# Graph-network layer on Trainium2: kept partial sums added to by adding transfers, eight rounds of unequal width, last round bank by bank

## The chip, the cores and the metric

One core of a Trainium2 chip runs the kernel. The metric is device time in microseconds (us) of the whole kernel, here of one launch on one core. The engines are PE (TensorE), DVE (VectorE), ACT (ScalarE), POOL (GpSimd) and SP (SyncE, which only issues transfers here). PEld is PE's weight load, which runs beside its products.

## The reference

12,500 nodes with 64 features, 400,000 edges (`src`, `dst`), three layers. Cut to what is computed:

```python
h = relu(layernorm(x))
for l in range(3):
    def mlp(z): return relu(z @ W1[l] + b1[l]) @ W2[l] + b2[l]
    msgs = mlp(h[dst])
    agg = segment_sum(msgs, src, num_segments=12500)
    h = mlp(h + agg)
out = x + h @ Wf + bf
```

A message depends only on the node it starts from, so each layer is a product of a matrix of edge counts (12,544 x 12,544 after padding) with the 12,544 messages, followed by the small MLP.

## The kernel before

**Counts.** The edge counts are small integers and are stored in device memory two to a byte (`counts_dram`). They are built once. The build has 49 columns of four groups, so 196 groups `k`. For each group DVE makes two one-hot tiles in `make_hots` (line 752: first the columns' tile, 128x832, here "cols", then the rows' tile, 128x4096, "rows"); POOL multiplies the first by the edges' weights (`weigh`, line 627); PE makes 32 small products (line 1307); ACT copies them out of PSUM (line 1132); DVE transposes the copy (line 760) two groups later; SP stores it. There are two slots for one-hots, so `make_hots(k)` waits until PE has used those of group k-2. Once every four groups, up to column 42, POOL also gathers edges for a later column (line 607).

**Layer 0.** The sums of layer 0 are made while the build runs. The result is split over seven stretches of 1792 nodes (a unit of work is one round for one stretch), each of four PSUM banks of 448 columns (one bank of one unit is called a job here). The build columns are taken in seven rounds of seven columns; round r needs the counts of its seven columns. A unit loads two chunks of counts from device memory (SP, line 450), DVE unpacks them into low and high halves (four instructions a unit, lines 791 and 799; 850 and 851 after the build), and PE multiplies: 14 products of 128x448 a job (line 1336). Between rounds the sum of each job is held in SBUF (`kept_sums`, in the tiles msg and arena): ACT copies it there (line 1141), and in the next round PE adds it back by a product with the identity in f32 (`add_kept`, line 1331) ahead of the job's own products. Unit u goes with build column u+8, one job a group, so that 41 of the 49 units run in the build; one more and the seven of the last round follow it. In these last ones the four banks run side by side over two chunks, and from the second stretch on PE also carries the MLP of the stretch before (`mlp_stage`, lines 1392, 1400, 1416) between them, ACT its activations (lines 1200, 1209, 1213), and DVE `read_sums` (lines 881 and 882, two instructions a bank) and `finish` (lines 894, 897).

**Layers 1 and 2** run from stored counts: seven stretches each, 5488 products in all on line 1438, with DVE unpacking (866, 867). The messages of each layer are scaled by their peak and split into two f16 parts (`upper_parts`, `lower_parts`); for layer 1 the peak goes through POOL (`share_peak`).

**Order.** All engines' programs are written out by hand in one order each; an engine runs its instructions in turn and waits on semaphores. SP's loads and stores share one queue.

The lines around which the change turns:

```python
if unit_of(j) >= 0:
    add_bank(unit_of(j), h)                    # PE, group k = 4j + h
t.matmul(ps[:, bank, 0:NB], ident[:], kept_sums(u % SB, b), start=True, stop=False)
```

## Time and profile before

| | us |
|---|---|
| Median of 3 runs (2256.7 to 2259.35) | 2258.89 |
| The profiled execution | 2256.61 |
| Its span | 2254.9 |
| up to the first rows' tile of the build | 64.1 |
| groups 0 to 31 of the build | 135.9 |
| groups 32 to 194, with layer 0 beside them | 742.9 |
| last group to the first product of the first whole unit after the build | 10.6 |
| two units without an MLP beside them | 28.7 |
| six stretches of the last round, with the MLP | 122.2 |
| layers 1 and 2 | 1150.5 |

A row of the timeline gives the start, the duration, the engine, the line of the kernel, the operation with what it writes and reads, and the idle time ahead of it with what ended that. Rows follow one another on an engine; a duration includes the fill and drain of the engine, so the pace of an engine is read from start to start.

### The profile page before, as it was taken

The page shows a single profiled execution, that of the slowest core. Times are in us where ns is not written, and L with a number is a line of the kernel's source. Part 1 is how long each engine was busy: PE and PEld are TensorE (multiplying, and loading weights), DVE is VectorE, ACT ScalarE, POOL GpSimd, SP SyncE. Part 2 cuts the span into 40 slices and gives each one's busy share as a digit, 9 for nine tenths or more (in the row PEclk, how much of TensorE's full clock was granted, in tenths as well). Part 3 has the DMA queues.
Part 4 walks back from the last instruction along what each step waited for, and adds up shares of the span by engine and source line. Part 5 has one row for each costly group of instructions (what it writes and reads, how often), then busy time and mean ns, then how long its engine had stood idle before and what let it go on. Part 6 is the DMA issues. An engine that isn't in the chain of part 4 may idle for free.

```text
span 2254.9 us, 39446 instructions
## 1 busy us (share of the span) xinstructions
PE 2096.7 (93%) x15866; PEld 1153.6 (51%) x15866; DVE 1512.7 (67%) x1683; ACT 663.7 (29%) x1632; POOL 643.7 (29%) x287
## 2 busy tenths in 40 slices
PE   3566779999999999999997999999999999999998
PEld 3444445555555555545553555555555555555554
DVE  7899999999999999846645434444463443444344
ACT  4885655555555555411200000000010000000000
POOL 3666667777767776500000000000000000000000
PEclk8796999999999999999998999999999999999999
DMA  7256666666666666642343435444444554555552
GB/s 194 71 139 180 178 181 189 182 188 196 190 188 193 185 187 176 186 125 72 122 127 110 146 111 160 151 128 145 143 132 134 157 165 126 169 159 159 145 157 68
DMA packets 332824, 344.46 MB, mean 153 GB/s; under 512 B 21562, under 2 KB 303992, under 8 KB 332184
## 3 DMA queue, kind: packets, MB, share of 16 engines
q1 hardware_dynamic: 327516, 335.59, 50.6%
q0 software_dynamic: 2352, 6.43, 1.1%
q8 instruction: 94, 1.54, 0.3%
q10 hardware_dynamic: 2816, 0.53, 0.2%
q14 instruction: 46, 0.38, 0.0%
HBM read 252.58 MB, written 89.89 MB: 152 GB/s over the span
## 4 chain that ended last, share of the span: by engine, by line
PE 80%; DVE 13%; issue 4%; DMA 2%; SPq 0%; ACT 0%; POOL 0%; DVEq 0%; POOLq 0%
PE ps L1438 46%; PE ps L1336 18%; DVE arena L752 6%; PE ps L1331 5%; PE ps L1307 5%; PE ps L1400 2%; DVE arena L760 2%; PE ps L1392 2%; PE ps L1416 1%; DMA arena<-counts_dram 1%; DVE arena L791 1%; DVE arena L799 1%; DVE arena L725 1%; SPq L439 0%; DVE msg L778 0%
## 5 line engine op out<-in xcount | busy, mean ns | idle before, releaser
L1438 PE MATMUL ps<-arena,parts 128*128 128x448 fp8e4 x5488 | 1054.0, 353 | 11.9 <-DVE arena L882 11.9
L1438 PEld LDWEIGHTS ps<-arena,parts 128*128 128x128 f16 x5488 | 535.1, 98 | 531.4 <-issue 44.7
L627 POOL TENSOR_TENSOR arena<-arena,weight_now 128x416 int32<-128x416 int32 x196 | 540.8, 2759 | 274.0 <-DVE arena L752 273.3
L866 DVE TENSOR_SCALAR arena<-arena 128x3136 uint16<-128x3136 uint16 x196 | 191.5, 977 | 624.5 <-PE ps L1438 617.9
L1336 PE MATMUL ps<-arena,parts 128*128 128x448 fp8e4 x2744 | 554.9, 353 | 1.5 <-DVE parts L832 1.5
L752 DVE TENSOR_TENSOR arena<-row_iota,key_now 128x4096 f16<-128x4096 f16 x196 | 446.3, 2277 | 0.0
L1336 PEld LDWEIGHTS ps<-arena,parts 128*128 128x128 f16 x2744 | 267.1, 98 | 296.9 <-issue 83.1
L1132 ACT ACTIVATE arena<-ps 128x800 uint16<-128x800 f32 x392 | 332.3, 874 | 73.2 <-PE ps L1307 64.1
L1200 ACT ACTIVATE arena<-ps,b1s 128x448 f32<-128x448 f32 x42 | 26.6, 634 | 943.5 <-PE ps L1392 943.5
L1307 PE MATMUL ps<-arena 128*128 128x53 fp8e4 x6272 | 204.3, 189 | 79.8 <-DVE arena L752 41.2
L1307 PEld LDWEIGHTS ps<-arena 128*128 128x128 f16 x6272 | 187.7, 98 | 151.4 <-DVE arena L752 95.5
L619 POOL COPY hT<-arena 128x896 f32 (+1 forms) x14 | 13.2, 945 | 699.5 <-ACT arena L1209 699.5
L760 DVE STREAM_TRANSPOSE arena<-arena 128x800 int32<-128x800 int32 x196 | 195.2, 996 | 3.7 <-DMA counts_dram<-arena 3.7
L867 DVE TENSOR_SCALAR arena<-arena 128x3136 uint16<-128x3136 uint16 x196 | 190.0, 969 | 0.0
L647 POOL PARTITION_ALL_REDUCE good<-good x1 | 0.4, 409 | 526.8 <-DVE good L1000 526.8
L752 DVE TENSOR_TENSOR arena<-word_iota,key_now 128x832 uint16<-128x832 f16 x196 | 113.5, 579 | 4.6 <-ACT weight_now L1111 4.6
L1141 ACT ACTIVATE msg<-ps 128x448 f32<-128x448 f32 x84 | 45.7, 544 | 163.7 <-PE ps L1336 163.7
L1331 PE MATMUL ps<-msg,ident 128*128 128x448 f32 x168 | 83.2, 577 | 3.0 <-DVE arena L851 3.0
L1331 PE MATMUL ps<-arena,ident 128*128 128x448 f32 x168 | 83.1, 576 | 0.0
L1141 ACT ACTIVATE arena<-ps 128x448 f32<-128x448 f32 x84 | 45.7, 544 | 118.9 <-PE ps L1336 118.9
L607 POOL DMA_INDIRECT arena<-edges_dram,start_i x49 | 76.5, 1562 | 8.0 <-issue 3.5
L791 DVE TENSOR_SCALAR arena<-arena 128x3136 uint16<-128x3136 uint16 x82 | 76.2, 930 | 3.1 <-DMA arena<-counts_dram 3.0
(127 smaller groups left out, 1146.9 us busy)
## 6 DMA issues: line engine op xcount, KB each, us to landing
arena<-counts_dram SPq DMA_DIRECT2D x294, 784.0 KB, 4.6
counts_dram<-arena SPq DMA_DIRECT2D x784, 100.0 KB, 2.2
h_dram<-parts SPq DMA_DIRECT2D x2, 1536.0 KB, 7.2
edges_dram<-arena SPq DMA_DIRECT2D x2, 1400.0 KB
arena<-in_x_dram SPq DMA_DIRECT2D x14, 192.0 KB
out_dram<-arena SPq DMA_DIRECT2D x14, 192.0 KB
arena<-in_dst_dram SPq DMA_DIRECT2D x1, 1400.0 KB
arena<-in_src_dram SPq DMA_DIRECT2D x1, 1400.0 KB
```

The costliest lines, as they stand in the source:

```text
L627: nc.gpsimd.tensor_tensor(pairs, pairs, weight_now[:, h * HW:(h + 1) * HW].unsqueeze(2).to_broadcast([P, HW, WORDS // 2]), ALU.mult).then_ ...
L752: return v.tensor_tensor(out, numbers.rearrange("p (m two) -> p m two", two=2).unsqueeze(1).to_broadcast(shape), key.unsqueeze(2).to_broad ...
L760: v.transpose(ctile[:, k % 2, :].bitcast(I32), stage[:, k % 2, :].bitcast(I32)).then_inc(s["counts_turned"], 1)
L791: v.tensor_scalar(spread[:, n % WIDE, 0, :].bitcast(U16), ring0[:, n % RING0, :].bitcast(U16), 0x0F0F, None, ALU.bitwise_and).then_inc(s[" ...
L866: v.tensor_scalar(spread[:, c % WIDE, 0, :].bitcast(U16), packed, 0x0F0F, None, ALU.bitwise_and)
L867: v.tensor_scalar(spread[:, c % WIDE, 1, :].bitcast(U16), packed, 4, 0x0F0F, ALU.logical_shift_right, ALU.bitwise_and).then_inc(s["counts_ ...
L1132: a.activation(to, product(q)[:, :, 0:2 * LP].rearrange("p c (m two) -> p c m two", two=2), ACT.Copy, scale=1.0 / WEIGHT_UNIT)
L1141: a.activation(kept_sums(u % SB, b), ps[:, bank, 0:NB], ACT.Copy).then_inc(s["sums_kept"], 1)
L1307: last = t.matmul(product(q)[:, c, 0:COLS], hot_r[:, slot, w, :], hot_c8[:, slot, w, 0:COLS], start=True, stop=True)
L1331: t.matmul(ps[:, bank, 0:NB], ident[:], kept_sums(u % SB, b), start=True, stop=False)
L1336: last = t.matmul(ps[:, bank, 0:NB], parts[:, (ROUND * (u // SB) + c) * CK + k, :], spread[:, c, b // 2, at:at + NB].bitcast(F8), start=u ...
L1438: last = t.matmul(ps[:, b, 0:NB], parts[:, c * CK + k, :], spread[:, c % WIDE, b // 2, at:at + NB].bitcast(F8), start=start, stop=stop)
```

## The change

Four things change in layer 0 and one at the start.

1. **Rounds.** There are eight rounds of 7, 7, 7, 7, 7, 6, 5 and 3 columns (`COLUMNS`), so 56 units and 224 jobs instead of 49 and 196. The number of products stays 2744. `spread_jobs` gives each of the first 196 jobs (`KEPT`) a build group: at most one seven-column job a group in round 0; then by a credit that gains 16 a group and pays twice the columns of a job. 179 jobs with 2406 products have a group of the build (before: 164 jobs with 2296), 17 of the seventh round follow it, then the 28 jobs of the last round. In rounds 1 to 4 every seventh or eighth group has two jobs (26 groups in all have two), and three or four groups at the start of rounds 2, 3 and 4 have none. DVE unpacks and SP loads by tables that follow from this (`unpack_group`, `load_group`): 180 unpacks in the build instead of 164; 26 groups have two.
2. **Kept sums.** PE no longer adds them. ACT copies a job's sum, scaled, into one of four stages (`sums_stage`), and POOL issues a transfer from that stage to the kept sum that adds (`add_sums`, `accum_op`). The 28 jobs of round 0 are copied to their kept place, and a transfer adds 64 rows of `hT` to each; 168 further transfers move 128 rows of 448 f32. A transfer of group k-1's job is issued behind `weigh(k)`, and ahead of the gather. `row_edges` becomes 8 bits wide, which makes room for the stages.
3. **Last round.** Its jobs are run bank after bank with six products each, with MLP stages between (`MLP_AT`). `read_sums` adds the kept sum in one instruction a bank, 28 instead of 56. Its first call waits for all adding transfers.
4. **Scale of layer 1.** The peak is turned and spread by two small products of PE rather than by POOL, after stretch 4's place in the order instead of after all.
5. **Start.** ACT keeps the first keys ahead of the square root and of `make_h0(0)`.

The diff, cut to its core:

```diff
+COLUMNS = (7, 7, 7, 7, 7, 6, 5, 3)
+ROUNDS = len(COLUMNS)
+FROM = [sum(COLUMNS[:r]) for r in range(ROUNDS + 1)]
 UNITS = ROUNDS * SB
-AHEAD = KG + 1
-FUSED = BUILD - AHEAD
+JOBS = UNITS * SBB
+KEPT = JOBS - SB * SBB
+CREDIT = 16
+STAGES = 4
...
+def spread_jobs():
+    groups, credit = [], 0
+    for k in range(BUILD * HG):
+        credit = 2 * KG if len(groups) < SB * SBB else min(credit, 2 * KG) + CREDIT
+        while len(groups) < KEPT:
+            r = len(groups) // (SB * SBB)
+            if k < HG * (FROM[r + 1] + 1) or credit < 2 * COLUMNS[r]:
+                break
+            credit -= 2 * COLUMNS[r]
+            groups.append(k)
+    return groups + [BUILD * HG] * (JOBS - len(groups))
+JOB_GROUP = spread_jobs()
+IN_LOOP = JOB_GROUP.index(BUILD * HG)
+def jobs_with(k):
+    return [n for n in range(IN_LOOP) if JOB_GROUP[n] == k]
+def unpack_group(n):
+    return max(JOB_GROUP[n - 1] if n else 0, JOB_GROUP[n] - 1)
+def load_group(n):
+    u, c = n // ROUND, n % ROUND
+    at = max(JOB_GROUP[u * SBB] - HG + c, HG * FROM[u // SB + 1])
+    if n >= RING0:
+        u, c = (n - RING0) // ROUND, (n - RING0) % ROUND
+        at = max(at, unpack_group(u * SBB + 2 + c) - 1)
+    return min(at, BUILD * HG)
...
-        row_edges = sb("row_edges", [P, BUILD * QN, QW], F16)
+        row_edges = sb("row_edges", [P, BUILD * QN, QW], U8)
+        sums_stage = sb("sums_stage", [P, STAGES, NB], F32)
...
+        def tiles_of(u, c):
+            n = COLUMNS[u // SB]
+            return 2 * FROM[u // SB] + c * n, n
...
+            for k in range(BUILD * HG):
+                if k in (3 * HG, 6 * HG):
+                    store_h0(k // (6 * HG))
+                while load_group(loaded) <= k:
+                    load_round(loaded)
+                    loaded += 1
+                store_counts(k)
+            for n in range(loaded, ROUND * UNITS):
...
+            def add_sums(n):
+                u, b = n // SBB, n % SBB
+                pool.wait_ge(s["sums_kept"], n + 1)
+                if u < SB:
+                    own = slice(b // 2 * D, b // 2 * D + D)
+                    pool.dma_start(kept_sums(u, b)[own], hT[own, u * SBH + b % 2 * NB:u * SBH + b % 2 * NB + NB],
+                                   accum_op=ALU.add).then_inc(s["rows_added"], 16)
+                else:
+                    if n == SB * SBB:
+                        pool.wait_ge(s["rows_added"], 16 * SB * SBB)
+                    pool.dma_start(kept_sums(u % SB, b), sums_stage[:, n % STAGES, :], accum_op=ALU.add).then_inc(
+                        sums_added[n % STAGES], 16)
...
+                for n in jobs_with(k - 1):
+                    add_sums(n)
...
+            def unpack_step(n):
+                u, c = n // SBB, n % ROUND
+                m = u * ROUND + c
+                size = tiles_of(u, c)[1] * SBH
+                packed = ring0[:, m % RING0, 0:size].bitcast(U16)
+                if n % SBB < 2:
+                    dve.wait_ge(round_loaded[m % RING0], 16 * (m // RING0 + 1))
+                    if u:
+                        dve.wait_ge(s["sums_done"], SBB * (u - 1) + 2)
+                    v.tensor_scalar(spread[:, c, 0, 0:size].bitcast(U16), packed, 0x0F0F, None, ALU.bitwise_and).then_inc(
+                        s["low_unpacked"], 1)
+                else:
+                    if u:
+                        dve.wait_ge(s["sums_done"], SBB * u)
+                    v.tensor_scalar(spread[:, c, 1, 0:size].bitcast(U16), packed, 4, 0x0F0F, ALU.logical_shift_right,
+                                    ALU.bitwise_and).then_inc(s["counts_unpacked"], 1)
...
+                    if l == 0:
+                        if i == 0 and b == 0:
+                            for added in sums_added:
+                                dve.wait_ge(added, 16 * (KEPT - SB * SBB) // STAGES)
+                        if i:
+                            dve.wait_ge(s["u_done"], 2 * (i - 1) + b % 2 + 1)
+                        v.scalar_tensor_tensor(zP[:, b * NB:(b + 1) * NB], ps[:, b, 0:NB], scal[:, 0, 6:7], kept_sums(i, b),
+                                               ALU.mult, ALU.add).then_inc(s["sums_read"], 1)
+                        continue
...
+            for n in range(unpacked, KEPT + SBB):
+                unpack_step(n)
+            for i in range(SB - 1):
+                n = KEPT + SBB * (i + 1)
+                read_sums(0, i, (0, 1))
                 if i >= 2:
                     finish(0, i - 2, 0)
+                unpack_step(n)
+                unpack_step(n + 1)
+                read_sums(0, i, (2, 3))
+                if i >= 2:
                     finish(0, i - 2, 1)
-                if i < SB - 1:
-                    unpack_tail(n + 2)
-            find_peak(1, BLOCKS + EARLY_PEAKS[1], EARLY_PEAKS[1])
+                    if 2 * (i - 1) == EARLY_PEAKS[1]:
+                        find_peak(1, BLOCKS + EARLY_PEAKS[1], EARLY_PEAKS[1])
+                unpack_step(n + 2)
+                unpack_step(n + 3)
+            reduce_peak(1)
+            make_scale(1)
+            finish(0, SB - 3, 0)
+            finish(0, SB - 3, 1)
+            lower_parts(1, 0)
             unpack(0, 1, 0, 0)
-            make_scale(1)
-            for n in range(4):
+            for n in range(1, 4):
...
+            act.wait_ge(s["variance_made"], 1)
+            a.activation(stat[:, 2, :], stat[:, 1, :], ACT.Sqrt).then_inc(s["root_made"], 1)
+            act.wait_ge(s["norm_made"], 1)
+            make_h0(0)
...
-            def keep_sums(u, b, bank):
-                act.wait_ge(s["sums_done"], SBB * u + b + 1)
-                if u < SB and b < 2:
-                    act.wait_ge(s["parts_made"], ROUND * (u + 1))
-                a.activation(kept_sums(u % SB, b), ps[:, bank, 0:NB], ACT.Copy).then_inc(s["sums_kept"], 1)
+            def keep_sums(n):
+                u, b = n // SBB, n % SBB
+                act.wait_ge(s["sums_done"], n + 1)
+                if u < SB:
+                    if b < 2:
+                        act.wait_ge(s["parts_made"], ROUND * (u + 1))
+                    to = kept_sums(u, b)
+                else:
+                    if n >= SB * SBB + STAGES:
+                        act.wait_ge(sums_added[n % STAGES], 16 * (n // STAGES - SB * SBB // STAGES))
+                    to = sums_stage[:, n % STAGES, :]
+                a.activation(to, ps[:, b % 2, 0:NB], ACT.Copy, scale=scal[:, 0, 6:7]).then_inc(s["sums_kept"], 1)
...
-            def add_kept(u, b, bank):
-                t.matmul(ps[:, bank, 0:NB], ident[:], kept_sums(u % SB, b), start=True, stop=False)
-            def multiply_chunk(u, c, b, bank, stop):
-                for k in range(CK):
-                    at = k * SBH + b % 2 * NB
-                    last = t.matmul(ps[:, bank, 0:NB], parts[:, (ROUND * (u // SB) + c) * CK + k, :],
-                                    spread[:, c, b // 2, at:at + NB].bitcast(F8), start=u < SB and c == 0 and k == 0,
-                                    stop=stop and k == CK - 1)
-                return last
-            def add_bank(u, b):
-                if b == 0:
-                    pe.wait_ge(s["parts_made"], ROUND * (u // SB + 1))
-                if SBB * u + b >= 2:
-                    pe.wait_ge(s["sums_kept"], SBB * u + b - 1)
+            def add_bank(n):
+                u, b = n // SBB, n % SBB
+                bank = b if n >= KEPT else b % 2
+                if n % (SB * SBB) == 0:
+                    pe.wait_ge(s["parts_made"], -(-2 * FROM[u // SB + 1] // CK))
+                if n < 2:
+                    pe.wait_ge(s["hidden0_kept"], BLOCKS)
+                elif n < KEPT:
+                    pe.wait_ge(s["sums_kept"], n - 1)
+                elif n < KEPT + 2:
+                    pe.wait_ge(s["sums_kept"], KEPT)
+                elif n == KEPT + 2:
+                    pe.wait_ge(s["scale_made"], 1)
+                elif n == KEPT + 3:
+                    pe.wait_ge(s["keys_kept"], 2 * BUILD)
                 else:
-                    pe.wait_ge(s["hidden0_kept"], BLOCKS)
-                if u >= SB:
-                    add_kept(u, b, b % 2)
+                    pe.wait_ge(s["sums_read"], n - KEPT - SBB + 1)
                 for c in range(ROUND):
+                    first, tiles = tiles_of(u, c)
                     pe.wait_ge(s["low_unpacked" if b < 2 else "counts_unpacked"], ROUND * u + c + 1)
-                    last = multiply_chunk(u, c, b, b % 2, c == ROUND - 1)
+                    for k in range(tiles):
+                        at = k * SBH + b % 2 * NB
+                        last = t.matmul(ps[:, bank, 0:NB], parts[:, first + k, :], spread[:, c, b // 2, at:at + NB].bitcast(F8),
+                                        start=c == 0 and k == 0, stop=c == ROUND - 1 and k == tiles - 1)
...
-            MLP_AT = {1: (0,), 2: (1,), 3: (2,), 5: (3,), 7: (4, 5)}
-            for u in range(FUSED, UNITS):
-                i = u - (UNITS - SB)
-                for c in range(ROUND):
-                    pe.wait_ge(s["counts_unpacked"], ROUND * u + c + 1)
-                    if c == 0 and u % SB == 0:
-                        pe.wait_ge(s["parts_made"], ROUND * (u // SB + 1))
-                    for b in range(SBB):
-                        if c == 0:
-                            if u == FUSED:
-                                pe.wait_ge(s["sums_kept"], SBB * FUSED if b < 2 else SBB * (FUSED - 1))
-                            elif i <= 0:
-                                pe.wait_ge(s["sums_kept"], SBB * FUSED + b + 1)
-                            else:
-                                pe.wait_ge(s["sums_read"], SBB * (i - 1) + b + 1)
-                            add_kept(u, b, b)
-                        last = multiply_chunk(u, c, b, b, c == ROUND - 1)
-                        if c == ROUND - 1:
-                            last.then_inc(s["sums_done"], 1)
-                        elif b == SBB - 1:
-                            last.then_inc(s["counts_used"], 1)
-                        if i >= 1:
-                            for n in MLP_AT.get(c * SBB + b + 1, ()):
-                                mlp_stage(0, i - 1, n)
+            MLP_AT = ((0, 1), (2,), (3,), (4, 5))
+            for n in range(IN_LOOP, JOBS):
+                add_bank(n)
+                i, b = n // SBB - (UNITS - SB), n % SBB
+                if i >= 1:
+                    for stage_n in MLP_AT[b]:
+                        mlp_stage(0, i - 1, stage_n)
+                if i == SB - 1 and b == 0:
+                    turn_peak(1)
+                if i == SB - 1 and b == 1:
+                    spread_peak(1)
```

POOL's queue in the build, at a place with one job a group and one with two. Before:

```order
L627 TENSOR_TENSOR arena<-arena,weight_now 128x32x13 [waits cols_made,keys_kept] x4
L607 DMA arena<-edges_dram,start_i 128x256 [waits keys_turned]
L627 TENSOR_TENSOR arena<-arena,weight_now 128x32x13 [waits cols_made,keys_kept] x4
L607 DMA arena<-edges_dram,start_i 128x256 [waits keys_turned]
L627 TENSOR_TENSOR arena<-arena,weight_now 128x32x13 [waits cols_made,keys_kept] x4
```

After:

```order
L671 TENSOR_TENSOR arena<-arena,weight_now 128x32x13 [waits cols_made,keys_kept]
L688 DMA msg<-sums_stage 128x448 [waits sums_kept]
L671 TENSOR_TENSOR arena<-arena,weight_now 128x32x13 [waits cols_made,keys_kept]
L688 DMA arena<-sums_stage 128x448 [waits sums_kept]
L651 DMA arena<-edges_dram,start_i 128x256 [waits keys_turned]
L671 TENSOR_TENSOR arena<-arena,weight_now 128x32x13 [waits cols_made,keys_kept]
L688 DMA arena<-sums_stage 128x448 [waits sums_kept]
L688 DMA msg<-sums_stage 128x448 [waits sums_kept]
L671 TENSOR_TENSOR arena<-arena,weight_now 128x32x13 [waits cols_made,keys_kept]
```

Behind each multiplication by the weights (line 671 now) stand one or two adding transfers that wait for ACT's copy, and the gather (line 651) stands behind them.

PE's queue in one stretch of the last round. Before:

```order
L1336 MATMUL ps<-arena,parts 128x448 x7
L1331 MATMUL ps<-msg,ident 128x448
L1336 MATMUL ps<-arena,parts 128x448 x7
L1392 MATMUL ps<-arena,W1s 64x448 x2
L1331 MATMUL ps<-msg,ident 128x448
L1336 MATMUL ps<-arena,parts 128x448 x7
L1392 MATMUL ps<-arena,W1s 64x448 x2
L1331 MATMUL ps<-arena,ident 128x448
L1336 MATMUL ps<-arena,parts 128x448 x7
L1400 MATMUL ps<-arena,W2b 128x448 x2
L1331 MATMUL ps<-arena,ident 128x448
L1336 MATMUL ps<-arena,parts 128x448 x14
```

After:

```order
L1419 MATMUL ps<-arena,parts 128x448 x6
L1465 MATMUL ps<-arena,W1s 64x448 x4
L1419 MATMUL ps<-arena,parts 128x448 x6
L1473 MATMUL ps<-arena,W2b 128x448 x2
L1419 MATMUL ps<-arena,parts 128x448 x6
L1473 MATMUL ps<-arena,W1b 128x448 x2
L1419 MATMUL ps<-arena,parts 128x448 x6
L1489 MATMUL ps<-W2b,arena 128x128 x7
```

The identity products (1331) are gone, and six products stand between two stages of the MLP.

ACT's queue at the start of the build. Before:

```order
L1087 ACT_TABLE_LOAD
L1087 ACTIVATE stat<-stat 128x98
L1092 ACTIVATE parts<-msg,stat 128x64 x8
L1100 COPY keys_row<-arena 128x256
L1101 ACTIVATE rk_now<-arena,row_base 128x128
L1109 COPY key_now<-ps 128x256
L1111 CAST weight_now<-ps 128x64
```

After:

```order
L1161 COPY keys_row<-arena 128x256
L1162 ACTIVATE rk_now<-arena,row_base 128x128
L1170 COPY key_now<-ps 128x256
L1172 CAST weight_now<-ps 128x64
L1170 COPY key_now<-ps 128x256
L1172 CAST weight_now<-ps 128x64
L1179 ACT_TABLE_LOAD
L1179 ACTIVATE stat<-stat 128x98
L1153 ACTIVATE parts<-msg,stat 128x64 x16
```

The keys (`keys_row`, `key_now`, `weight_now`), for which DVE's first one-hots wait, now come ahead of the normalisation (`stat`) and of h0 (`parts`).

## Rows read from the trace of the kernel before

**Rows 1.** Busy time by stage: stage, length, us (and instructions) of PE, PEld, DVE, ACT, POOL, clock, DMA share, GB/s.

```profile
199.93:942.86 742.93, 707.13 (x7880) 404.08 (x7878) 739.86 (x668) 434.95 (x1069) 513.40 (x198) 0.99 0.64 186
942.86:953.47 10.61, 7.62 (x64) 3.83 (x63) 6.89 (x8) 3.90 (x10) 2.83 (x1) 0.98 0.78 239
953.47:982.19 28.72, 28.72 (x129) 14.55 (x129) 10.37 (x13) 2.17 (x4) 0.00 (x0) 0.95 0.55 166
982.19:1104.39 122.20, 122.20 (x565) 62.17 (x565) 68.48 (x101) 27.49 (x45) 5.97 (x7) 1.00 0.29 88
```

**Rows 2.** Timeline, one group of the build, DVE and POOL.

```profile
604.13 0.58 DVE L752 TENSOR_TENSOR arena<-word_iota,key_now 128x832 uint16<-128x832 f16 x1
...
604.63 2.28 DVE L752 TENSOR_TENSOR arena<-row_iota,key_now 128x4096 f16<-128x4096 f16 x1
...
604.85 2.82 POOL L627 TENSOR_TENSOR arena<-arena,weight_now 128x416 int32<-128x416 int32 x1 [1.66 <-DVE arena L752]
...
606.83 1.00 DVE L760 STREAM_TRANSPOSE arena<-arena 128x800 int32<-128x800 int32 x1
...
607.76 0.93 DVE L791 TENSOR_SCALAR arena<-arena 128x3136 uint16<-128x3136 uint16 x1
...
608.61 0.58 DVE L752 TENSOR_TENSOR arena<-word_iota,key_now 128x832 uint16<-128x832 f16 x1
```

**Rows 3.** Chain that ended last, same group: start, us that it adds, what.

```profile
603.29 0.99 PE ps L1307 x32
604.29 0.84 PE ps L1331 x2
605.12 2.65 PE ps L1336 x14
```

**Rows 4.** Busy time by stage, early part of layer 0, no kept sums to add yet.

```profile
200.00:300.00 100.00, 75.79 (x940) 44.59 (x937) 99.19 (x94) 60.48 (x148) 67.67 (x26) 0.96 0.63 180
```

**Rows 5.** Timeline, PE and ACT in one stretch of the last round.

```profile
1043.29 0.92 PE L1331 MATMUL ps<-msg,ident 128*128 128x448 f32 x2
...
1044.04 1.49 PE L1336 MATMUL ps<-arena,parts 128*128 128x448 fp8e4 x7
...
1051.72 1.67 PE L1400 MATMUL ps<-arena,W2b 128*128 128x448 f32 x4
...
1052.67 1.39 ACT L1209 ACTIVATE arena<-ps,b2s 128x448 f32<-128x448 f32 x2 [2.38 <-PE ps L1400]
```

**Rows 6.** Timeline, POOL's gathers and DVE's instructions beside POOL, start of the run.

```profile
46.64 1.30 POOL L607 DMA_INDIRECT arena<-edges_dram,start_i  x1
...
47.06 0.17 DVE L714 TENSOR_SCALAR start_f<-start_f 128x7 f32<-128x7 f32 x1
...
47.53 0.38 DVE L714 TENSOR_SCALAR start_f<-start_f 128x7 f32<-128x7 f32 x1
...
49.50 0.95 POOL L607 DMA_INDIRECT arena<-edges_dram,start_i  x1 [0.30 <-issue]
...
66.28 1.29 DVE L752 TENSOR_TENSOR arena<-word_iota,key_now 128x832 uint16<-128x832 f16 x1
```

**Rows 7.** Timeline, a gather beside an unpack in the build.

```profile
616.73 0.93 DVE L799 TENSOR_SCALAR arena<-arena 128x3136 uint16<-128x3136 uint16 x1
...
616.80 1.70 POOL L607 DMA_INDIRECT arena<-edges_dram,start_i  x1 [0.16 <-issue]
```

**Rows 8.** Timeline, the first one-hot tile of the build.

```profile
63.57 0.59 DVE L752 TENSOR_TENSOR arena<-word_iota,key_now 128x832 uint16<-128x832 f16 x1 [4.64 <-ACT weight_now L1111]
```

**Rows 9.** DVE's waits, 190 to 945 us: us in total, times, longest.

```profile
DVE arena L791 <- DMA arena<-counts_dram: 3.0, 6, 0.8
```

**Rows 10.** The gathers' line: time from issue to landing.

```profile
DMA to landing us min/median/max: 2.5/4.7/6.6
```

**Rows 11.** Groups of instructions, 199.93 to 942.86 us: busy us, mean ns, idle before.

```profile
L1141 ACT ACTIVATE arena<-ps 128x448 f32<-128x448 f32 x80 | 43.5, 544 | 113.1 <-PE ps L1336 113.1
```

161 lines of the change are left out of this document (55 added, 106 removed).

## Prediction

> **What bounds the kernel now.** I read the busy times by stage first, to see which engine is never idle in each stage, then the timeline of one group and of one stretch, to see the pace from start to start, and then POOL's rows, since the change puts work on it.
>
> In the build with layer 0 beside it DVE is busy for 739.86 of 742.93 us [rows 1]. One group takes 4.48 us on DVE, start to start: 0.50 for the columns' tile, 2.20 for the rows' tile, 0.93 for the transpose, 0.85 for one unpack [rows 2]. PE needs as much: 0.99 for the counts' products, 0.84 for the kept sum, 2.65 for 14 products [rows 3]. The chain runs through PE there, but DVE has no gap either, so PE's relief alone cannot shorten a group. Behind the build PE is the bound: it is busy for all of 28.72 and 122.20 us, DVE for 68.48 of the last [rows 1]. There each us taken from PE counts until DVE, ACT or a wait comes up. POOL's multiplication lasts 2.82 us but mostly waits: it starts 0.22 us into the rows' tile and ends at 607.67, 0.76 after that tile's end at 606.91 [rows 2]. The work itself is some 0.76 us.
>
> **Start.** DVE waits 4.64 us for the first keys [rows 8]. They no longer stand behind ACT's eight h0 instructions, whose input DVE itself makes last. DVE can begin at once, but ACT is late next: it has 16 of these instructions in a row ahead of the first copies of counts. The bounds are 0 and -4.6; I take -3.5, near the wait shown, because ACT too begins earlier.
>
> **The build.** DVE's tiles and transposes stay. Unpacks: before 164 x 0.85 = 139.4 us. After: 140 of seven columns x 0.85 = 119.0, 28 of six and 12 of five. An unpack is 0.82 us for its bytes and 0.03 fixed by my split of 0.85 (estimate), so 0.735 and 0.62, which gives 20.6 and 7.4. In all 147.0, so **+7.6**. PE falls to 0.99 plus 8/7 x 2.65 = 4.0 us a group in rounds 1 to 4, against 3.63 + 8/7 x 0.85 = 4.60 on DVE: PE's 0.84 a group is hidden by DVE and worth nothing here. Two jobs in one group cost PE 0.99 + 5.30 = 6.3, once in seven or eight groups; two one-hot slots give it the slack of more than a group. PE's clock: with PE at 75.79% the granted share is still 0.96 [rows 4], at the upper level of 2.4 GHz nearly throughout, so only the three pauses of three or four groups without jobs can let it fall to 1.2 GHz, and PE's slack covers that.
>
> **POOL and its port.** POOL's queue becomes: multiply, one or two adding transfers, sometimes the gather. The next multiplication stands behind them. The trace has no adding transfer. A gather issues in 0.95 us alone [rows 6] and in 1.70 beside an unpack, ending at 618.50, 0.84 after the unpack's end at 617.66 [rows 7]. An adding transfer starts about 0.9 after the rows' tile ends, as this gather does, and ends 1.9 to 2.6 after it; two end by 3.6. POOL then waits for the next rows' tile anyway, which ends 4.6 later. So the issue itself is hidden; the cover is gone only above some 3.6 us of issue a group. What isn't hidden is what the port costs DVE, at two places.
>
> (a) In 26 groups DVE has two unpacks, in 23 of them with an adding transfer. If POOL gets its turn between them and holds on for all of its issue, the second unpack is 0.84 late: 23 x 0.84 = 19.3. If it holds on as in the row where a small DVE instruction took 0.38 beside a gather, against 0.17 for its like: 23 x 0.21 = 4.8 [rows 6].
>
> (b) In 32 groups the gather stands behind an adding transfer. If that ends later than the next columns' tile (2.27 after the rows' tile), the gather waits for the whole next rows' tile, and the multiplication behind it meets an unpack and then holds up the next columns' tile, which then takes 1.29 instead of 0.58 [rows 6, 2]: 32 x 0.71 = 22.7. By the ends above the gather comes at 2.05 to 2.8, so it is near either way; in the five groups with two transfers it surely is late: 5 x 0.71 = 3.6.
>
> Together the bounds are +8.4 and +42.0; nothing in it can give a gain. I take **+8.4**, since the only row of a DVE instruction beside a gather's issue shows a short hold.
>
> The Trainium skill speaks against the change here: "SBUF — State Buffer", section "Who interferes with whom", says that the pair of ports that DVE and GpSimd share is an exclusive lock held for the whole instruction, and the section on the two sides of SBUF that descriptors of GpSimd's transfers cannot be written while DVE runs in a two-port mode. The first agrees with the columns' tile of 1.29 us in the trace; for a transfer's issue it would make the term +42. It is the first rival below.
>
> **The transfers themselves.** 168 of 229 KB and 28 of half that in all, 164 whole ones' worth in the build. The DMA share is 0.64 at 186 GB/s there, so all 16 engines give some 291 GB/s and a whole one costs 0.79 us of them [rows 1]. That is 130 us on top of 475 in about 750: 0.81 busy. If reading the old sum too doubles the price, 0.98. DVE waits for loads for 3.0 us in six places now [rows 9]; I double that: **+3.0**. Loads are issued two groups ahead, 9 us.
>
> **Behind the build.** Now: 10.61 + 28.72 + 122.20 = 161.5 us from the last rows' tile to layer 1 [rows 1]. After:
> - the first stage as before, 10.6, since DVE's last transposes still wait for stores; one of the 17 late jobs falls in it
> - 16 jobs of ten products; 2.65 / 14 = 0.189 each [rows 3]: 30.2
> - 0.8 for ACT's last copy, 0.54 and the way there and back [rows 11]
> - the first stretch of the last round, 24 x 0.189: 4.5
> - the wait for the last adding transfer: copy 0.6, issue 0.95, landing 4.7 as a gather's median [rows 6, 10], and 0.5 for the read, less the 5.3 that lie beside it: 1.5
> - six stretches. One now takes 122.20 / 6 = 20.37 us [rows 1]; it loses 32 of 56 products (6.05) [rows 3] and four kept sums of 0.75, 1043.29 to 1044.04 (3.0) [rows 5]: 11.3 each, 67.9
> - DVE's queue ahead of layer 1 (scale, a finish, lower parts, an unpack, then the reads) is longer than the one stretch of PE beside it: 3.0, estimate
>
> That is 118.5, so **-43.0**. DVE is not the bound of a stretch: 68.48 / 6 = 11.4 now, less the eight read instructions that become four and four unpacks cut to 6/14. The scale by PE instead of POOL, and the 13 us in which DVE judges the counts after layer 1's first stretch, change nothing that PE waits for.
>
> **Sum.** 2256.6 - 3.5 + 7.6 + 8.4 + 3.0 - 43.0 = 2229.1 for an execution like the profiled one. That one lies 2.3 below the median of the runs, 2258.89, so 2231.
>
> **Rivals.**
> 1. *The port is held for all of each issue.* For it: the multiplication that waits for the rows' tile to the end, and the 1.29. Against: the 0.38. Both (a) and (b) at full price: 2231 + 33.6 = 2265, slower by 0.3%. It decides if the second unpack of a group is late by 0.84 rather than 0.2 and the gather falls behind the columns' tile.
> 2. *The adding transfers fill the DMA engines*, so that loads and stores land late and DVE waits in every group: slower. In the build (750 - 475) = 275 us of all engines are free for 164 transfers, 1.68 each, 2.1 times the plain price. At three times: 475 + 389 = 864, so 114 more: 2345. For it: a transfer that adds reads twice, and the share is 0.64 already. Against: the transfers lie within SBUF, in long rows of 1792 bytes.
> 3. *The stretches become a chain of hand-overs.* Between two stages of the MLP stood 7 to 14 products and a kept sum; now six products, 1.1 us. ACT finishes its pair 2.34 after the stage begins (1051.72 to 1054.06), PE's stage (1.67 with its drain) and six products take 2.6 to 2.8 [rows 5]. It is covered by 0.3 at least. If 0.8 shows at three hand-overs of six stretches, 14.4: 2246.
> 4. *PE's relief does shorten the build*, if DVE's start to start hides waits for PE: at most a few us, 2225. DVE's parts add up to the whole, so this has little for it.
>
> **How the numbers follow.** The forecast, 2231, 55%. Rival 1 14%, rival 2 11%, rival 3 13%, rival 4 and a cheaper start or tail 4%, other losses 3%. The range leaves out rival 2 and the far ends of the others: 2213 (start -4.6, no port or DMA cost, shorter waits in the tail) to 2267 (rival 1 with its spread). A measurement of this kernel tells 0.2%, 4.5 us, from no change. Faster by more: the forecast, rivals 3 and 4: 71%. Within: part of rivals 1 and 3: 8%. Slower: rival 2, the rest of rival 1 and other losses: 21%.
>
> **What would show it.** Groups of 3.63 + 0.85 per unpack on DVE in the build, unpacks of 0.93 with none near 1.8, and columns' tiles of 0.58 with few of 1.29; POOL idle ahead of most multiplications; last rows' tile near 955; stretches of 11 to 12 us with PE idle only ahead of the second; a DMA share in the build of 0.8 to 0.9. The prediction is wrong if columns' tiles or unpacks are stretched in most groups, if DVE waits for counts every group, or if PE is idle between the stages of the MLP.

## The result, and the profile after

Four runs of the changed kernel have a median of 2278.94 us (2276.58 to 2285.01), beside 2259.12 of the kernel before: a ratio of 1.0094, 95% interval 1.0073 to 1.0115. It is slower by 0.9%, where 2231 us and a gain of 1.2% were forecast; the time lies above the range. The profiled execution is the slowest of the four (2285.01, span 2283.2), 6.1 us above their median, and that of the kernel before lies 2.5 below its own; so 8.5 us of the difference between the two traces, 28.3, belong to these two executions.

Busy time by stage of the changed kernel, columns as in [rows 1]: up to group 32 of the build, the build from there with layer 0 beside it, the last transposes, the 16 late jobs, the first stretch of the last round, the rest up to layer 1, layers 1 and 2.

```profile
0.00:197.47 197.47, 103.82 (x1328) 88.24 (x1328) 176.96 (x285) 135.72 (x411) 113.11 (x71) 0.81 0.55 144
197.47:997.10 799.63, 639.93 (x7725) 381.51 (x7722) 766.84 (x682) 455.58 (x1085) 609.15 (x374) 0.94 0.89 222
997.10:1010.30 13.20, 7.38 (x67) 3.91 (x66) 6.64 (x8) 4.54 (x10) 6.32 (x5) 0.95 1.07 272
1010.30:1044.36 34.06, 33.29 (x160) 16.22 (x161) 11.19 (x17) 10.14 (x16) 13.52 (x15) 0.92 0.97 223
1044.36:1053.26 8.90, 4.70 (x25) 2.28 (x25) 2.94 (x7) 0.00 (x0) 0.98 (x1) 1.00 0.84 191
1053.26:1127.33 74.07, 68.68 (x329) 36.46 (x330) 44.73 (x80) 28.42 (x46) 5.59 (x6) 0.98 0.29 90
1127.33:2283.20 1155.87, 1131.62 (x5910) 584.68 (x5910) 508.19 (x611) 58.72 (x94) 8.33 (x10) 0.99 0.46 139
```

The build takes 799.63 us where it took 742.93 [rows 1]. Two columns say why. DVE is busy 27.0 us longer, 766.84 for 739.86. And it is now idle for 32.8 us, where it was for 3.1. The DMA share has gone from 0.64 to 0.89. Behind the build the four rows add up to 130.2 us, from 161.5.

The last row is 5.4 us longer than before, and 3.0 of these lie at the very end. There POOL goes through a closing drain, an instruction of its sequencer, and the kernel ends 0.24 us after it. First of the changed kernel, then of the kernel before (the number is its duration in ns):

```profile
L159 POOLq DRAIN  x1: 7073/7073/7073, 2275.9 to 2275.9; - x1
...
L113 POOLq DRAIN  x1: 4074/4074/4074, 2250.6 to 2250.6; - x1
```

DVE's groups of instructions in the build, shapes apart, and its wait for loads (us in total, times, longest):

```profile
L856 DVE TENSOR_SCALAR arena<-arena 128x3136 uint16<-128x3136 uint16 x69 | 73.5, 1071 | 28.2 <-DMA arena<-counts_dram 27.9
L861 DVE TENSOR_SCALAR arena<-arena 128x3136 uint16<-128x3136 uint16 x70 | 70.0, 1000 | 0.0
...
DVE arena L856 <- DMA arena<-counts_dram: 32.2, 27, 3.9
```

The seven-column unpack averages 1.07 and 1.00 us, not 0.93; and the six waits of 3.0 us of before [rows 9] have become 27 of 32.2. The timeline of DVE shows such a wait:

```profile
519.24 1.00 DVE L821 STREAM_TRANSPOSE arena<-arena 128x800 int32<-128x800 int32 x1
524.18 0.98 DVE L856 TENSOR_SCALAR arena<-arena 128x3136 uint16<-128x3136 uint16 x1 [3.93 <-DMA arena<-counts_dram]
```

The DMA queues in the build, first of the changed kernel, then of the kernel before: q0 carries what POOL issues (packets, MB, share of 16 engines); then issues, KB each, median us to landing.

```profile
q0 software_dynamic: 25038, 41.46, 30.6%
...
counts_dram<-arena SPq DMA_DIRECT2D x652, 100.0 KB, 3.6
arena<-counts_dram SPq DMA_DIRECT2D x68, 784.0 KB, 7.3
msg<-sums_stage POOLq DMA_DIRECT2D x74, 224.0 KB, 6.0
```

```profile
q0 software_dynamic: 1680, 4.59, 2.3%
...
counts_dram<-arena SPq DMA_DIRECT2D x652, 100.0 KB, 2.2
arena<-counts_dram SPq DMA_DIRECT2D x81, 784.0 KB, 5.2
```

Queue q0 holds 30.6% of 799.6 us, or 244.7 us of all 16 engines; the gathers held 2.3% of 742.9, or 17.1. The build has 148 whole adding transfers and 28 half ones, so 162 whole ones: (244.7 - 17.1) / 162 = 1.40 us each, where the prediction had 0.79. A load takes 7.3 us to land, from 5.2; a store 3.6, from 2.2. Their packets themselves are no slower: the loads' packets of 896 bytes take 0.048 us on average in both kernels, the stores' of 3200 bytes 0.176 before and 0.171 now. So the loads and stores are late because they queue. ACT, which must wait for a free stage, does so only twice, 3.3 us in all.

Why some unpacks are long is in the timelines of POOL (first four rows) and DVE in one group:

```profile
212.37 0.83 POOL L683 DMA_DIRECT2D msg<-hT  x1 [1.47 <-ACT msg L1211]
213.50 2.67 POOL L651 DMA_INDIRECT arena<-edges_dram,start_i  x1 [0.30 <-issue]
216.17 0.93 POOL L671 TENSOR_TENSOR arena<-arena,weight_now 128x416 int32<-128x416 int32 x1
217.00 1.05 POOL L683 DMA_DIRECT2D arena<-hT  x1
...
212.93 2.29 DVE L813 TENSOR_TENSOR arena<-row_iota,key_now 128x4096 f16<-128x4096 f16 x1
215.13 1.01 DVE L821 STREAM_TRANSPOSE arena<-arena 128x800 int32<-128x800 int32 x1
216.06 1.88 DVE L856 TENSOR_SCALAR arena<-arena 128x3136 uint16<-128x3136 uint16 x1
```

The adding transfer's issue puts the gather behind the next columns' tile. The gather starts inside the rows' tile, so it stands until the tile has ended (215.22) and ends 0.95 later, at 216.17. The multiplication behind it starts just when DVE starts its unpack, which takes 1.88 us, 0.95 too long: the multiplication's own 0.93. In the build 17 of DVE's instructions (15 unpacks, two columns' tiles) are stretched by over 0.3 us, 15.5 us in all. Beside each of them runs a multiplication; in 14 cases it stands directly behind a gather, and 12 of these gathers had waited for a rows' tile as this one did. Gathers that start just ahead of a rows' tile, by 0.03 us say, take 1.07 us and wait for nothing.

The issue of an adding transfer by itself hardly stretches anything of DVE's. Here one lies inside a rows' tile, POOL's row and DVE's:

```profile
482.17 0.91 POOL L688 DMA_DIRECT2D msg<-sums_stage  x1 [1.48 <-ACT sums_stage L1211]
...
482.12 2.29 DVE L813 TENSOR_TENSOR arena<-row_iota,key_now 128x4096 f16<-128x4096 f16 x1
```

Neither is longer than alone. Of the 139 seven-column unpacks, 93 have an issue and nothing else of POOL's beside them: they take 0.945 us on average (1.10 at most), and 0.952 the 29 with nothing beside them. But an unpack holds up the issue. Here the issue starts 0.14 us ahead of the unpack, POOL's row and DVE's:

```profile
236.02 1.18 POOL L683 DMA_DIRECT2D arena<-hT  x1
...
236.16 0.93 DVE L856 TENSOR_SCALAR arena<-arena 128x3136 uint16<-128x3136 uint16 x1
```

In 42 such cases (the issue up to 0.2 us ahead) every issue ends 0.10 to 0.13 us after the unpack. Issues with no unpack beside them take 0.87 us on average; the 79 that end in this way 1.07.

Behind the build, PE's timeline: the 16 late jobs, the first two stretches, and two later ones, which start 11.55 us apart; last DVE's first read of kept sums.

```profile
1010.30 33.29 PE L1419 MATMUL ps<-arena,parts 128*128 128x448 fp8e4 x160 [5.27 <-DVE arena L856]
1044.36 4.70 PE L1419 MATMUL ps<-arena,parts 128*128 128x448 fp8e4 x24 [0.77 <-ACT sums_stage L1211]
1053.26 2.25 PE L1419 MATMUL ps<-arena,parts 128*128 128x448 fp8e4 x6 [4.20 <-DVE arena L856]
...
1077.31 1.30 PE L1419 MATMUL ps<-arena,parts 128*128 128x448 fp8e4 x6
...
1088.86 1.30 PE L1419 MATMUL ps<-arena,parts 128*128 128x448 fp8e4 x6
...
1051.42 1.28 DVE L936 SCALAR_TENSOR_TENSOR arena<-ps,scal,msg 128x448 f32<-128x448 f32 x2 [5.97 <-DMA arena<-sums_stage]
```

### The profile page after: what moved, and what is told of

The parts are those of the page before. It is cut to its first block, busy times and chain, and to the rows that moved or that the text cites. A ratio compares the mean times of both kernels' runs of the same rounds, so it can differ in the third digit from the quotient of the medians.

```text
span 2283.2 us, 39388 instructions
## 1 busy us (share of the span) xinstructions
PE 1989.4 (87%) x15534; PEld 1113.3 (49%) x15534; DVE 1517.5 (66%) x1684; ACT 693.1 (30%) x1660; POOL 757.0 (33%) x482
## 4 chain that ended last, share of the span: by engine, by line
PE 57%; DVE 22%; DMA 9%; issue 7%; SPq 3%; POOL 1%; ACT 1%; DVEq 0%; POOLq 0%; ACTq 0%
PE ps L1511 45%; DVE arena L813 11%; DMA arena<-counts_dram 8%; DVE arena L821 4%; PE ps L1419 4%; SPq L489 2%; PE ps L1473 2%; DVE arena L861 2%; DVE arena L856 2%; PE ps L1465 2%; DMA counts_dram<-arena 1%; PE ps L1489 1%; PE ps L1374 1%; POOL arena L671 1%; DVE arena L786 1%
## 5 line engine op out<-in xcount | busy, mean ns | idle before, releaser
L1511 PE MATMUL ps<-arena,parts 128*128 128x448 fp8e4 x5488 | 1056.0, 354 | 15.5 <-DVE arena L946 11.9
L921 DVE TENSOR_SCALAR arena<-arena 128x3136 uint16<-128x3136 uint16 x196 | 191.5, 977 | 622.6 <-PE ps L1511 622.2
L1419 PE MATMUL ps<-arena,parts 128*128 128x448 fp8e4 x2744 | 569.0, 361 | 12.6 <-DVE arena L856 10.9
L671 POOL TENSOR_TENSOR arena<-arena,weight_now 128x416 int32<-128x416 int32 x196 | 481.1, 2455 | 149.5 <-DVE arena L813 145.7
L1374 PE MATMUL ps<-arena 128*128 128x53 fp8e4 x6272 | 212.9, 192 | 212.9 <-DVE arena L813 90.0
L1374 PEld LDWEIGHTS ps<-arena 128*128 128x128 f16 x6272 | 198.4, 100 | 277.1 <-DVE arena L813 221.0
L922 DVE TENSOR_SCALAR arena<-arena 128x3136 uint16<-128x3136 uint16 x196 | 190.2, 970 | 0.0
L1211 ACT ACTIVATE sums_stage<-ps,scal 128x448 f32<-128x448 f32 x168 | 106.7, 635 | 197.1 <-PE ps L1419 193.6
L856 DVE TENSOR_SCALAR arena<-arena 128x3136 uint16<-128x3136 uint16 (+3 forms) x112 | 107.0, 965 | 51.5 <-DMA arena<-counts_dram 41.3
L861 DVE TENSOR_SCALAR arena<-arena 128x3136 uint16<-128x3136 uint16 (+3 forms) x112 | 97.8, 887 | 3.9 <-PE ps L1419 3.9
L688 POOL DMA_DIRECT2D arena<-sums_stage x84 | 85.2, 1014 | 41.1 <-ACT sums_stage L1211 36.9
L688 POOL DMA_DIRECT2D msg<-sums_stage x84 | 80.0, 952 | 52.1 <-ACT sums_stage L1211 47.3
L1197 ACT ACTIVATE row_edges<-ps 128x16 uint8<-128x16 f32 x392 | 74.5, 190 | 0.0
```

The source lines that it names most:

```text
L671: nc.gpsimd.tensor_tensor(pairs, pairs, weight_now[:, h * HW:(h + 1) * HW].unsqueeze(2).to_broadcast([P, HW, WORDS // 2]), ALU.mult).then_ ...
L688: pool.dma_start(kept_sums(u % SB, b), sums_stage[:, n % STAGES, :], accum_op=ALU.add).then_inc(sums_added[n % STAGES], 16)
L856: v.tensor_scalar(spread[:, c, 0, 0:size].bitcast(U16), packed, 0x0F0F, None, ALU.bitwise_and).then_inc(s["low_unpacked"], 1)
L861: v.tensor_scalar(spread[:, c, 1, 0:size].bitcast(U16), packed, 4, 0x0F0F, ALU.logical_shift_right, ALU.bitwise_and).then_inc(s["counts_un ...
L921: v.tensor_scalar(spread[:, c % WIDE, 0, :].bitcast(U16), packed, 0x0F0F, None, ALU.bitwise_and)
L922: v.tensor_scalar(spread[:, c % WIDE, 1, :].bitcast(U16), packed, 4, 0x0F0F, ALU.logical_shift_right, ALU.bitwise_and).then_inc(s["counts_ ...
```

## The experiments

Line numbers of the experiments' rows are those of their own kernels. Medians are of four to ten runs; the kernel before, on the same chips, has 2258.0 to 2259.5.

**Theories.** 1: the adding transfers fill the DMA engines, and DVE waits for loads. 2: POOL's new work holds the port that it shares with DVE; either each issue does so (2a), or only the gather that is now late does, with the multiplication behind it (2b). 3: the schedule of eight rounds itself costs the time.

### No adding transfers

```diff
 def add_sums(n):
-    u, b = n // SBB, n % SBB
-    pool.wait_ge(s["sums_kept"], n + 1)
...
+    pass
```

> The changed kernel with all 196 adding transfers left out, and the waits for them (the sums kept between rounds and the own rows' hT are not added, so part of the computation is missing); everything else, the schedule of eight rounds, the unpacks and the last round bank by bank, stays. Theory 1 (the adding transfers fill the 16 DMA engines, so that loads land late and DVE waits for them, and part of the stretched instructions is contention): the build falls from 799.6 us to about 750, DVE's waits for loads from some 30 us to 3, and the whole to about 2225. Theory 2 (POOL's issue holds the port that it shares with DVE): the same total, about 2230, since the issues are gone too; this run alone doesn't tell 1 from 2. Theory 3 (the schedule itself, its bursts of jobs and pauses of PE, costs the time): the build stays near 790 and the whole near 2275.

2223.43 us, ratio 0.9839 (0.9822 to 0.9855). The build and the stages up to layer 1:

```profile
197.77:952.12 754.35, 625.41 (x7723) 375.44 (x7721) 747.11 (x683) 455.14 (x1085) 511.44 (x198) 0.96 0.66 187
...
952.12:1069.56 117.44, 109.79 (x581) 58.11 (x580) 65.57 (x109) 43.52 (x72) 8.43 (x7) 1.00 0.40 121
```

Theory 3 falls. Without the transfers the change is worth 1.6%, the tail is 117.4 us and DVE's busy time 747.1. The transfers as a whole cost 55 us. Between the two traces the difference is 61.5, of which 19.7 us are DVE's busy time and 25.6 its idle time in the build, 12.8 lie behind the build, and 3.0 in POOL's drain at the end, which takes 4.07 us here as in the kernel before. What is left of theory 3 is 4 us: DVE waits 7.2 us for loads here, 3.0 before. It does so in five places, four of them 122 to 128 us apart (337, 459, 586 and 714 us), as the rounds are.

### Few bytes, or a copy in place of an addition

```diff
-pool.dma_start(kept_sums(u % SB, b), sums_stage[:, n % STAGES, :], accum_op=ALU.add).then_inc(
+pool.dma_start(kept_sums(u % SB, b)[:, 0:32], sums_stage[:, n % STAGES, 0:32], accum_op=ALU.add).then_inc(
```

(and the same for hT)

> The changed kernel, but each adding transfer moves only the first 32 of 448 columns of its rows (the other columns are not added, so part of the computation is missing). The number of transfers, their issues on POOL, their waits and the number of descriptors stay; the bytes fall to 1/14. Theory 1 (bytes on the DMA engines): DVE's waits for loads fall from some 30 us to below 8, the DMA share of the build from 0.89 to about 0.70, the unpack of seven columns keeps its 1.07 us; the build is some 25 to 30 us shorter than 799.6, the whole about 2250. Theory 2 (the port is held during POOL's issue): the stretched unpacks and the rest of DVE's extra 19 us of busy time stay, whatever becomes of the waits. If instead the unpacks fall to 0.93 as well, they are stretched by the transfers' traffic and not by their issue, and the whole comes near 2230. If reading and writing cost by descriptor and not by byte, the DMA share stays above 0.8 and nothing much is gained.

```diff
-pool.dma_start(kept_sums(u % SB, b), sums_stage[:, n % STAGES, :], accum_op=ALU.add).then_inc(
+pool.dma_start(kept_sums(u % SB, b), sums_stage[:, n % STAGES, :]).then_inc(
```

> The changed kernel, but the 168 transfers of kept sums copy where they added (the old sum is overwritten and lost, so part of the computation is missing); the 28 of hT still add. Bytes moved, issues and waits stay. Theory 1 in the form of its price (an adding transfer takes the DMA engines 1.39 us where a copy of the same bytes takes 0.79, because the old sum is read too): the queue of these transfers falls from 30.7% of the build to about 18%, the DMA share from 0.89 to about 0.77, DVE's waits for loads from some 30 us to below 10, the whole to about 2255. If the transfers cost the same without adding, it is the bytes and descriptors from SBUF to SBUF that cost, and the whole stays at 2279. Theory 2 (the issue holds the port): no difference, 2279, in either case.

Few bytes: 2251.34 us (ratio 0.9945 to 0.9973). Copies: 2254.53 (0.9962 to 0.9989). The build of each, and q0 in the build with copies:

```profile
195.94:975.21 779.27, 633.66 (x7718) 378.10 (x7719) 771.73 (x683) 453.87 (x1085) 605.35 (x374) 0.95 0.69 185
```

```profile
196.25:974.55 778.30, 630.39 (x7720) 377.03 (x7718) 766.25 (x683) 455.10 (x1085) 592.01 (x374) 0.96 0.77 229
...
q0 software_dynamic: 13328, 41.53, 17.2%
```

With few bytes the waits are gone (779.27 - 771.73 = 7.5 us, with no transfer at all 7.2), but DVE's busy time is even 5 us longer: 25 stretched instructions, some 24 us. The copies leave waits of 11.9 us, somewhat more than the 10 expected. So the bytes make the waits, and something that remains makes the stretching. Theories 1 and 2 both hold, each for about half of the build's loss.

The copies give the price. By the queue's account they move the same bytes, at 17.2% of the build for 30.6%: (0.172 x 778.3 - 17.1 - 14 x 1.40) / 148 = 0.66 us for a copy, 1.40 for an addition. The Trainium skill, "Collectives: The Full Stack", section "The bandwidth ceiling: the fold count and why AG ≠ RS ≠ AR", says of collectives that an adding transfer is slow because it has two sources to read, with two read descriptors per chunk on one ring, and gives a ratio of 1.93. The ratio of prices here, 2.1, agrees.

The number of packets, 25,038 for 13,328, shows something else. An adding transfer has one packet for each of its rows, 1792 bytes and 0.176 us on average; a copy has packets of two or three rows, 3584 bytes in 0.162 us and 5376 in 0.232. Smaller packets alone don't explain the price: the loads' packets of 896 bytes take 0.048 us, so two of them would move a row in 0.10 (an estimate, since they come from device memory). Most of the difference therefore goes with the adding. That its reason is the reading of the old sum is not shown by itself, since the profile counts the same bytes for both.

### The start alone

```diff
-            act.wait_ge(s["norm_made"], 1)
-            make_h0(0)
...
             keep_keys(0, 1)
...
+            act.wait_ge(s["norm_made"], 1)
+            make_h0(0)
```

> The kernel before with one part of the change alone: ACT's order at the start, the square root and h0 behind the first keys. Nothing is left out. If the gain at the start is kept (the first rows' tile ends 5.6 us earlier in the changed kernel, but at group 32 only 2.5 us of it are left), 2256.6, that is 2.5 us below the kernel before; by the prediction's term 3.5 below, 2255.6. If the seven rounds of before take it back fully, 2259.

2254.58 us, ratio 0.9985 (0.9976 to 0.9995): 3.6 below the kernel before, with an interval of 1.1 to 5.4. The prediction's -3.5 lies well inside. In the trace much of the gain is lost on the way: the first rows' tile starts 5.9 us earlier than before, that of group 32 4.6, the last one 2.3, and the span is 2.5 shorter.

### The gather ahead of the adding transfers

```diff
 weigh(k)
-for n in jobs_with(k - 1):
-    add_sums(n)
 if k % HG == 2 and k // HG + WR < WT:
     gather(k // HG + WR)
+for n in jobs_with(k - 1):
+    add_sums(n)
```

> The changed kernel with one pair of steps exchanged in POOL's queue: in every fourth group the gather of the next window stands ahead of the adding transfers of that group, not behind them. Nothing is left out. Background: in the changed kernel 13 gathers of the build start late, wait through a whole rows' tile of DVE, and the multiplication behind each falls beside an unpack, which then takes 1.87 us where 0.94 is its own (14 to 15 us in all; 23 us with short transfers). Theory 2b (the late gather and the multiplication behind it hold DVE up, and the issue of an adding transfer by itself holds nothing): the stretched unpacks go, DVE's busy time in the build falls from 766.8 to about 750, the build by 12 to 16 us, the whole to about 2265. Theory 2a (any issue of POOL's beside an unpack stretches it): the stretching only moves to the adding transfers behind the gather, 2279. The waits for loads (some 30 us) stay or grow by some us under both, since the DMA engines have the same work in less time.

> The gather ahead of the adding transfers, and these move only the first 32 of 448 columns (the other columns are not added, so part of the computation is missing). It answers to the run with short rows alone, 2251.3 us, and to the run without any transfer, 2223.4. Theory 2b (late gathers hold DVE up, issues don't): nearly all that was left goes, DVE's busy time in the build falls from 771.7 to about 749, the whole to about 2228. Theory 2a (any issue beside an unpack stretches it): it stays near 2250. What lies between 2223.4 and this run is then the price of 196 issues, waits and descriptors with hardly any bytes in them.

> The changed kernel with the gather ahead of the adding transfers of its group, and the 168 transfers of sums copy where they added (the old sum is lost, so part of the computation is missing); bytes written, issues and waits stay. It completes the square: with the gather late, adding 2278.9, copying 2254.5, hardly any bytes 2251.3; with the gather first, adding 2276.5, hardly any bytes 2230.2. If the DMA engines are full only when the old sum is read too, so that the late gathers' cost was hidden behind them, this run gains the whole price of the late gathers: 2234 to 2238. If a copy's bytes alone fill them already, the waits for loads come up as they did with the gather first and adding, and it stays at 2248 to 2254.

With whole additions 2276.53 us, with few bytes 2230.16, with copies 2241.91. The builds, in this order:

```profile
195.06:987.67 792.61, 640.39 (x7721) 380.28 (x7722) 753.95 (x682) 456.42 (x1086) 619.00 (x374) 0.95 0.89 224
```

```profile
194.93:953.61 758.68, 628.04 (x7724) 375.37 (x7721) 750.98 (x682) 456.21 (x1085) 612.75 (x374) 0.96 0.71 190
```

```profile
196.33:960.10 763.77, 628.45 (x7723) 376.89 (x7721) 750.70 (x682) 455.06 (x1085) 603.39 (x374) 0.96 0.78 233
```

Theory 2b holds for the stretching, and 2a falls. The exchange of two steps takes 12.9 us from DVE's busy time with whole additions, 15.6 with copies and 20.8 with few bytes, though the same number of issues stays. With whole additions 4 stretched instructions are left of 17. One gather of the build, with DVE's unpack a little later, shows the cure:

```profile
209.78 1.61 POOL L651 DMA_INDIRECT arena<-edges_dram,start_i  x1 [0.17 <-issue]
211.39 0.93 POOL L683 DMA_DIRECT2D msg<-hT  x1
...
214.60 0.93 DVE L856 TENSOR_SCALAR arena<-arena 128x3136 uint16<-128x3136 uint16 x1
```

But the time of the first run missed its forecast of 2265: the gain is 2.4 us, inside the intervals. In the two traces the build is 7.0 us shorter, not 12.9. DVE's waits for loads rose from 32.2 us to

```profile
DVE arena L856 <- DMA arena<-counts_dram: 38.0, 30, 2.7
```

and the share stayed at 0.89. The copies came to 2241.9, between the two values on record for them (2234 to 2238 and 2248 to 2254). The six runs in one table, medians in us:

| | whole additions | copies | few bytes |
|---|---|---|---|
| gather behind the adding transfer | 2278.9 | 2254.5 | 2251.3 |
| gather ahead of it | 2276.5 | 2241.9 | 2230.2 |
| gain | 2.4 | 12.6 | 21.1 |

The fuller the DMA engines (0.89, 0.77, 0.69), the less a faster DVE gains: 2.4 of 12.9 us, 12.6 of 15.6, and all of 20.8. With whole additions it asks for its loads sooner, and waits 5.8 us more in the trace; the other 4.6 us between 7.0 and 2.4 are no more than the spread of the runs. With both causes away only 6.7 us are left against the kernel without transfers, and 2.9 of them are POOL's drain (6.95 us for 4.07). So neither loss can be read off by undoing the other.

### PE adds part of the sums

The gather first; PE adds the kept sum in jobs that stand alone in their group, 83 of 151 in one kernel and 99 in the other. `uS` holds a scaled identity here.

```diff
+if n in BY_PE:
+    t.matmul(ps[:, bank, 0:NB], uS[:, 0:P], kept_sums(u % SB, b), start=True, stop=False)
```

> The changed kernel with the gather first, and with PE adding the kept sum back (a product with a scaled identity, as the kernel before does it) in 83 of the 151 jobs of the build that add; ACT then copies the result straight to its place. 85 adding transfers of sums stay, in the groups with two jobs and behind the build, and the 28 of hT. Nothing is left out. Theory 1 and 2b together (each adding transfer costs the DMA engines 1.39 us, and PE has some 0.6 us a group to spare): the DMA share of the build falls from 0.89 to about 0.79, DVE's waits for loads from some 30 us to 10 or less, the build from 799.6 to about 760 us; the whole to about 2240, below the kernel before. Theory 3 (PE is the next bound: 0.84 us for each kept sum in a group, on top of bursts of two jobs): DVE waits for sums in its unpacks, the build stays above 780 and the whole near 2260.

> The same with PE adding in all 99 jobs that stand alone in their group; 69 adding transfers of sums stay. Nothing is left out. From the sums of PE (0.99 + 2.65 + 0.84 = 4.48 us for a group with one job, as much as DVE, and 6.3 for one with two) PE falls up to 9 us behind DVE's tiles before each pause, where it is up to 7 in the kernel with 83. If the DMA engines are what counts, this gains 2 to 4 us more than that kernel, about 2237. If PE is the bound, its time behind DVE shows as DVE's waits for sums in the unpacks, and it is slower than that kernel, 2245 to 2260.

Both 2253.4 us (ratios 0.9981, interval 0.9970 to 0.9992, and 0.9980, 0.9969 to 0.9990): better than both kernels, but not the 2240 and 2237 that were expected. The build and the tail of the first, whose profiled execution is the slowest of its ten (2260.7):

```profile
195.07:973.17 778.10, 691.33 (x7891) 410.11 (x7889) 754.10 (x682) 452.48 (x1086) 557.57 (x292) 0.96 0.78 205
...
973.17:1102.28 129.11, 114.36 (x579) 58.96 (x578) 65.41 (x109) 42.80 (x70) 25.28 (x26) 0.96 0.57 147
```

The share falls to 0.78 as forecast. The waits for loads fall to 19.4 us, not to 10, 4 us of waits for PE come up, and the tail keeps its 129 us, since its jobs still use transfers. In the second kernel the share is 0.75, the waits for loads are 15.9 us and those for PE 4.4, and the time is the same: the 16 transfers less bring nothing that shows. At the same share of 0.78 the copies with the gather first waited 13.0 us, this kernel 19.4, in 18 places all over the build. Why so much waiting is left with half of the transfers is not shown; of the adding transfers that stay in the build, most (52 in both kernels) belong to the groups with two jobs, where they stand close together.

### A version that beats both

The kernel before with the new start. ACT scales the sixth round's sums as it copies them, 28 half-size adding transfers add hT late in the build, and in the last round DVE adds the kept sum as it reads.

```diff
-                            add_kept(u, b, b)
+                            if i < 0:
+                                add_kept(u, b, b)
...
+                    if l == 0:
+                        v.scalar_tensor_tensor(zP[:, cols], ps[:, b, 0:NB], scal[:, 0, 6:7], kept_sums(i, b),
+                                               ALU.mult, ALU.add).then_inc(s["sums_read"], 1)
```

> A version built on the kernel before: its seven rounds and PE's adding back of the kept sums in rounds one to five, with the changed start order, and of the rest of the change only what takes work from PE behind the build. ACT scales the sums of the sixth round as it copies them; 28 adding transfers of half size put the own rows' hT to them, late in the build; in the last round PE no longer adds the kept sum, DVE adds it as it reads (four instructions a stretch where there were eight). Nothing is left out. What is saved: seven stretches lose four kept sums of 0.75 us each, 21 us, and the start gives 3.6 (the run of it alone). What it costs by the finding that an adding transfer's bytes on the DMA engines matter: 14 whole ones' worth of 1.39 us in a build with a DMA share of 0.64, hardly a wait. So about 2234, faster than the kernel before by 1.1%, and than the changed kernel by 2.0%. If the adding transfers as such (their issue, their waits) are what makes the changed kernel slow, it comes to 2245 or more; if PE is not the bound behind the build, to 2254.

2237.99 us, ratio 0.9908 (0.9892 to 0.9925): faster than the kernel before by 0.9%, than the changed one by 1.8%. The build and the stages up to layer 1, and PE at two points one stretch apart:

```profile
195.73:940.50 744.77, 707.67 (x7880) 404.34 (x7878) 740.12 (x668) 436.50 (x1069) 537.62 (x219) 0.99 0.66 188
940.50:1082.31 141.81, 137.31 (x700) 70.40 (x699) 69.45 (x96) 34.14 (x59) 15.23 (x15) 0.98 0.46 134
```

```profile
1032.19 0.97 PE L1415 MATMUL ps<-arena,W1s 128*64 128x448 f32 x4
...
1049.37 0.97 PE L1415 MATMUL ps<-arena,W1s 128*64 128x448 f32 x4
```

A stretch takes 17.18 us where it took 20.37, and the tail 141.8 for 161.5. The build is 1.8 us longer than before: 28 small transfers at a share of 0.66 cost little there (4.6 us of waits for loads, from 3.0). They cost 2.3 us in POOL's drain at the end, 6.36 for 4.07.

## Why the prediction was wrong

The step that failed is the price of the adding transfers: on the DMA engines (+3.0, which came to +29.2) and, by what an issue pushes behind it in POOL's queue, on DVE (+8.4, which came to +19.7). The tail added a smaller miss. In the order of the prediction's steps, with what each measured:

- **What bounds the kernel.** Right: DVE in the build, PE behind it. What the sum lacked is a third bound, the DMA engines, which it saw (share 0.64) and priced too low.
- **Start, -3.5.** Right, as far as it can be told: -3.6 by the run of it alone, 1.1 to 5.4.
- **Unpacks, +7.6.** Right: the kernel without transfers has 747.11 us of DVE's busy time for 739.86, +7.3.
- **Port, +8.4 taken of +8.4 to +42.** The term came to +19.7. The failing step is the choice between the ends. Part (a), the issue between two unpacks, did not happen: an issue holds nothing of DVE's and is itself held by the unpack, so 0.38 against 0.17 [rows 6], which lay beside a gather, was the wrong likeness. Part (b), the gather behind the adding transfer, happened as described and at more than its price: the multiplication mostly met the unpack itself, 0.95 us, and only twice a columns' tile. The text had called it near either way and counted 5 of 32; 12 came, and two more multiplications behind gathers that had not waited. These 14 and three others make 15.5 us; the other 4 are small amounts that no single row explains. Rival 1 expected both parts at full price; (b) came, (a) did not. The page that it cites (the Trainium skill, "SBUF — State Buffer", section "Who interferes with whom") tells of a lock held for the whole instruction. The trace agrees for the multiplication, whose whole 0.93 us are in the unpack's 1.88, but not for an issue: where it starts first, it does not hold the unpack. The prediction's other sentence from that page, that descriptors of POOL's transfers can't be written while DVE runs in a two-port mode, agrees with the 42 issues that end 0.10 to 0.13 us after the unpack.
- **DMA lateness, +3.0.** The largest miss in the build: +29.2 (waits 32.2 for 3.0), of which 25 go with the bytes and 4 with the schedule, where they stand without any transfer. The term rested on 0.79 us for a transfer, from a mean rate. It is 1.40, where a copy is 0.66. The text allowed for that ("0.98 if doubled"), yet let the waits only double. Rival 2 set its deciding point at 2.1 times 0.79 us, where the mean share reaches one. But waits grow long before that. In the kernel before they are 3.0 us at a share of 0.64. With the new schedule they are 7.2 at 0.66, 7.5 at 0.69, 7.7 at 0.71, 11.9 at 0.77, 13.0 and 19.4 at 0.78 (the copies with the gather first, and PE adding in 83 jobs), 32 to 38 at 0.89. That it is the bursts of jobs, loads and stores that make it so is argued, not shown.
- **Tail, -43.0.** -31.3; without transfers -44.1, so the terms for PE's work were right (stretches of 11.55 for 11.3). Missed: 2.6 in the first stage, where the DMA share is shown as 1.07 and DVE waits 3.9 us for a store; 3.1 in the 16 jobs, whose 160 products take 33.29 us at a granted clock of 0.92, behind a pause of 5.27 (without transfers 30.43 at 1.00, behind 1.37); 2.9 in the first stretch, where DVE waits 5.97 us for the last adding transfer and PE stands for 4.20, of which 1.5 were foreseen; 3.2 in the rest.
- **Rival 3** did not come: PE's waits in a stretch are 0.44 us. **Rival 4** neither.

In sum the sign turned because two terms of the transfers, 11.4 us together in the build, came to 49, and the tail gave 12 less. That leaves 7 us of the 2285.0 of the profiled execution: 1 at the start (2.5 gained up to group 32 in place of 3.5), and layers 1 and 2 with 5.4 more, a term that the sum put at nothing. Of these, 3.0 are POOL's closing drain, 7.07 us for 4.07. Another 1.6 lie in the first stretch of layer 1, whose first 28 products take 7.14 us behind a pause of 3.62, not 5.5; they stand in the kernel without transfers too. The drain is 4.07 us in every kernel without adding transfers. It is 6.36 with the 28 small ones alone, 6.1 to 7.1 with the others that add, and 8.9 and 9.2 with the copies. Why it grows is not settled.

## What to carry over

A transfer that adds must be priced at about twice a copy (1.40 us for 0.66 here), and a mean DMA share of 0.9 is no room to spare: what counts is the wait of the next load, 32 us in all at that share. A new instruction in a queue costs what it pushes behind it: ask which queued instruction it moves into the time of another engine's, and put it behind that. An operation off the critical path (PE's kept sum, 0.84 us hidden under DVE) should stay where it is free, and be removed only where it is not.

## What was not expected of the hardware

- Adding in place from SBUF to SBUF, 128 rows of 1792 bytes: 1.40 us of all 16 engines, a copy of the same 0.66. An addition lands in 6.0 us (median) in the changed kernel, a copy in 4.3 in the run with the gather late.
- POOL's issue of an adding transfer did not by itself lengthen a DVE instruction by more than 0.2 us in the changed kernel. Inside a rows' tile it takes its own time (33 cases, 0.87 us on average); beside an unpack it mostly ends 0.10 to 0.13 us after it, and takes up to 1.65. An indirect gather that starts inside a rows' tile ends 0.95 us after that tile (2.67 us in the case above, up to 3.15).
- POOL's closing drain depends on what POOL issued in the first half of the run: 4.07 us without adding transfers, 6.1 to 9.2 with them, over 1100 us after the last one.
- The cost of an instruction's place hides when another resource is full: the same exchange of two steps gave 2.4, 12.6 and 21.1 us.
